# Splitting the down products of the shared groups of an FFN into three single-pass products

## What is computed

```python
x = x + 0.5 * ffn(layernorm(x))
x = x + attention(layernorm(x))        # 16 heads of 64, rotary and Fourier terms
x = x + 0.5 * ffn(layernorm(x))        # same weights again

def ffn(x):                            # N = 4096 tokens, E = 8 experts, top 2, 2 shared groups
    scores = softmax(x @ gate_w.T)
    comb = top-2 weights per token, with an expert's capacity of 1280 tokens
    g, u = x @ we_gate[e].T, x @ we_up[e].T          # every expert on every token, inner size 128
    y = sum_e comb[:, e] * ((silu(g) * u) @ we_down[e].T)
    shared = (silu(x @ ws_gate.T) * (x @ ws_up.T)) @ ws_down.T    # inner size 2 x 128
    return y + shared
```

## Time and profile before

| | |
|---|---|
| median of 3 runs | 1273.29 us (1272.16 to 1274.07) |
| profiled execution: its time | 1275.4 us |
| profiled execution: its span | 1273.6 us |
| granted clock of TensorE, share of full | 0.995 |
| first FFN, with attention's first steps | about 18 to 231 us of the span |
| attention | about 231 to 1084 us |
| second FFN | about 1084 to 1273.6 us |

### The profile page before, as it was taken

The page is one execution under the profiler, slowest core; times in us unless marked ns, Lnnn a source line. Parts: engine busy times, 40 slices in busy tenths (PEclk is TensorE's granted clock), DMA queues, the critical chain, the costliest instruction groups (busy, mean ns, idle before and its releaser), DMA issues.

```text
span 1273.6 us, 20947 instructions
## 1 busy us (share of the span) xinstructions
PE 1229.2 (97%) x7346; PEld 780.9 (61%) x7346; DVE 955.6 (75%) x1443; ACT 627.9 (49%) x917; POOL 896.2 (70%) x652
## 2 busy tenths in 40 slices
PE   4999999899999999999999999999999987999998
PEld 3666666556666566666666666666666644666665
DVE  6656777778888888888888888888787865656632
ACT  3444522455555546455556555555555552443422
POOL 0443346788998898898898899889889932543353
PEclk9999999999999999999999999999999998999999
DMA  5353150132333333232323232323232310443150
GB/s 169 134 183 91 43 150 17 33 66 54 70 58 67 61 64 64 63 65 59 69 60 68 60 68 60 68 57 70 51 77 52 76 19 19 141 142 108 43 158 17
DMA packets 118677, 95.35 MB, mean 75 GB/s; under 512 B 75760, under 2 KB 85008, under 8 KB 118320
## 3 DMA queue, kind: packets, MB, share of 16 engines
q1 hardware_dynamic: 118064, 93.75, 30.2%
q10 hardware_dynamic: 512, 0.26, 0.1%
HBM read 57.53 MB, written 2.88 MB: 47 GB/s over the span
## 4 chain that ended last, share of the span: by engine, by line
PE 86%; issue 4%; POOL 4%; DVE 3%; DMA 1%; ACT 1%; SPq 0%; POOLq 0%; DVEq 0%; ACTq 0%
PE banks L1156 16%; PE banks L453 15%; PE banks L1135 13%; PE banks L466 10%; PE banks L1074 6%; PE banks L994 5%; PE banks L1172 5%; PE banks L1140 4%; PE banks L1181 4%; PE banks L1002 3%; POOL work L1428 2%; PE banks L1113 1%; POOL turn L1418 1%; PE banks L415 1%; PE banks L408 1%
## 5 line engine op out<-in xcount | busy, mean ns | idle before, releaser
L1006 DVE TENSOR_REDUCE neg_max<-banks 128x2 f32<-128x1024 f32 x256 | 305.1, 1226 | 11.0 <-PE banks L994 6.2
L1256 ACT ACTIVATE work<-banks 128x1024 f32<-128x1024 f32 x256 | 262.4, 1026 | 93.8 <-PE banks L1140 77.6
L1156 PE MATMUL banks<-work 128*64 128x512 f32 x1024 | 233.8, 598 | 2.0 <-ACT work L1256 1.1
L1428 POOL TENSOR_TENSOR work<-work 128x1024 f32<-128x1024 f32 x64 | 159.6, 2494 | 81.4 <-PE banks L1156 81.3
L1418 POOL TENSOR_TENSOR turn<-turn,side_turned 128x512 f32<-128x512 f32 x128 | 163.7, 1301 | 29.8 <-DMA side_turned<-side 29.6
L1412 POOL TENSOR_TENSOR turn<-turn,fenc 128x512 f32<-128x512 f32 x128 | 162.8, 1291 | 2.0 <-DVE side L1327 2.0
L1423 POOL TENSOR_TENSOR qk_l<-turn,qk_h 128x512 fp32r<-128x512 f32 x128 | 161.8, 1285 | 2.8 <-ACT qk_h L983 2.8
L1156 PEld LDWEIGHTS banks<-work 128*64 128x64 f32 x1024 | 68.0, 136 | 135.0 <-issue 109.9
L1348 DVE TENSOR_TENSOR work<-work 128x1024 f32<-128x1024 f32 x64 | 105.4, 1647 | 38.2 <-PE banks L1156 38.2
L807 POOL TENSOR_TENSOR o_raw<-o_raw,work 128x512 f32<-128x512 f32 x52 | 66.9, 1289 | 89.8 <-DVE o_raw L723 89.7
L807 POOL TENSOR_TENSOR work<-work 128x512 f32<-128x512 f32 x44 | 56.5, 1292 | 96.7 <-DVE work L723 51.7
(11 more groups left out here) (177 smaller groups left out, 2459.3 us busy)
## 6 DMA issues: line engine op xcount, KB each, us to landing
work<-share SPq DMA_DIRECT2D x32, 1024.0 KB, 9.4
side_turned<-side SPq DMA_DIRECT2D x256, 128.0 KB, 3.1
rec_all<-rec_d SPq DMA_DIRECT2D x128, 128.0 KB, 3.0
x_tok<-in_x SPq DMA_DIRECT2D x8, 256.0 KB, 6.5
out<-x_tok SPq DMA_DIRECT2D x8, 256.0 KB, 9.4
work<-in_w_gate_up SPq DMA_DIRECT2D x1, 1280.0 KB, 7.2
work<-in_w_qk SPq DMA_DIRECT2D x1, 1024.0 KB, 9.7
den_d<-den_rows ACTq DMA_DIRECT2D x64, 4.0 KB
```

Of the source, the lines that this page charges most:

```text
L1006: return nc.vector.tensor_reduce(neg_max[:, g % 2, qt::DH], of, AX.X, ALU.max, negate=True)
L1156: ins = nc.tensor.matmul(o_bank(g)[OWN[h], :], v_all[:, kt, n * DH:(n + 1) * DH], pt[:, g % 2, kt, h * T:(h + 1) * T], start=(kt == 0), st ...
L1256: nc.scalar.activation(pt[:, g % 2, kt, :], S[kt].rearrange("p h q -> p (h q)"), ACT.Exp, scale=QSCALE).then_inc(s["probs"], 1)
L1428: nc.gpsimd.tensor_tensor(pt[:, g % 2, 2, :], pt[:, g % 2, 2, :], pt[:, g % 2, 3, :], ALU.add).then_inc(s["second_sum"], 1)
```

## The change

In units 20, 21, 30, 31, ..., 70, 71 of both FFNs (`split(i)`: batch 2 or later, shared group; 12 units in each FFN) the down product is made of three float32r products in place of one float32 product. ScalarE copies `hid(i)` to its high part `hid_hi[:, g]` (`hid_high`), GpSimd subtracts it from `hid(i)` for the low part `hid_lo[:, g]` (`hid_low`), and `down(i)` waits for the low part. ScalarE's copy stands right behind `silu(i)` in its queue and waits for `gated(i)`. The high part lies in the buffer `shift`, the low part in the third set of `qk_h`, both of them attention's. The down weights of the two shared groups are split once, at unit 9 of the first FFN, ScalarE making the high part and VectorE the low one. Attention's high part of its second head pair gets a wait for the down products that still read the low part's buffer.

```diff
@@ -53,6 +53,7 @@
 JOIN_NORM_AT = {p: (n,) for n, p in enumerate([p for p in range(26, 60) if p % 8 in (0, 1, 2, 6)], 1) if n < LN_STAGES}
 JOIN_TOKENS_AT, JOIN_FRONTS_AT, JOIN_LOGITS_AT = 61, 62, 63
 FOURIER_AT = 17
+DOWN_SPLIT_AT = 9
 
 
 def ffn_units():
@@ -100,6 +101,8 @@
         gu_hi = sb("gu_hi", [P, 2 * GROUPS, P], F32R)
         gu_lo = sb("gu_lo", [P, 2 * GROUPS, P], F32R)
         down_w = sb("down_w", [P, GROUPS, D])
+        down_hi = sb("down_hi", [P, NSH, D], F32R)
+        down_lo = sb("down_lo", [P, NSH, D], F32R)
         gate_w = sb("gate_w", [P, E])
         gate_hl = sb("gate_hl", [P, 2 * CB, GATE_ROWS], F32R)
         qk_hi = sb("qk_hi", [P, PAIRS, QK, P], F32R)
@@ -151,6 +154,7 @@
         qk_l = sb("qk_l", [P, SETS, QK, T], F32R)
         turn = sb("turn", [P, 2, QK, T])
         side = sb("side", [P, QK, T])
+        hid_lo = qk_h[:, 2]
         side_turned = sb("side_turned", [P, QK, T])
         route_room = side_turned[:].rearrange("p q t -> p (q t)")
         routing = lambda n: route_room[:, n * CT * E:(n + 1) * CT * E].rearrange("p (t e) -> p t e", e=E)
@@ -159,6 +163,7 @@
         neg_max = sb("neg_max", [P, 2, P])
         own_rows = sb("own_rows", [P, TT])
         shift = sb("shift", [P, 2, T], F32R)
+        hid_hi = shift
         ones_r = sb("ones_r", [P, P], F32R)
         ones_f = sb("ones_f", [P, 32])
         o_raw = sb("o_raw", [P, 2, T])
@@ -183,6 +188,7 @@
         in_first, in_fourier, in_x0, in_down = sem("in_first"), sem("in_fourier"), sem("in_x0"), sem("in_down")
         consts_ready = sem("consts_ready")
         w_hi_ready, w_lo_ready = sem("w_hi_ready"), sem("w_lo_ready")
+        down_hi_ready, down_lo_ready = sem("down_hi_ready"), sem("down_lo_ready")
         fenc_ps, fenc_ready = sem("fenc_ps"), sem("fenc_ready")
         dve_step = {ph: sem(f"dve_step_{ph}") for ph in ("setup", "f1", "att", "f2")}
         stored = sem("stored")
@@ -318,7 +324,7 @@
         def ffn(tag, last, share_d, follow=None):
             s = {n: sem(f"{tag}_{n}") for n in (
                 "normed", "xn_ready", "xn_first", "xt_ps", "x_hi_ready", "x_lo_ready", "logits_t", "logits_copied", "logits", "shifted", "exps", "masks", "pos",
-                "routed", "turned", "rows_ready", "gate_ps", "up_ps", "silu", "weighted", "gated", "down", "y_copied", "yt_ps", "x_done")}
+                "routed", "turned", "rows_ready", "gate_ps", "up_ps", "silu", "weighted", "gated", "hid_high", "hid_low", "down", "y_copied", "yt_ps", "x_done")}
             listed = tuple(sem(f"{tag}_listed{c}") for c in range(CHUNKS))
             in_share = tuple(tuple(sem(f"{tag}_in_share{n}{h}") for h in range(2)) for n in range(2))
             G, U, Y = (bank[0], bank[1]), (bank[2], bank[3]), (bank[4], bank[5])
@@ -359,6 +365,13 @@
             def experts(i):
                 return sum(1 for b, g in UNITS[0:i] if g >= NSH)
 
+            def split(i):
+                b, g = UNITS[i]
+                return b >= CB and g < NSH
+
+            def splits(i):
+                return sum(1 for n in range(i) if split(n))
+
             def last_of(b):
                 return max(i for i in range(N) if UNITS[i][0] == b)
 
@@ -455,7 +468,10 @@
 
                 def down(i):
                     b, g = UNITS[i]
-                    if g < NSH:
+                    if split(i):
+                        pe.wait_ge(s["hid_low"], splits(i + 1))
+                        pe.wait_ge(down_lo_ready, 1)
+                    elif g < NSH:
                         pe.wait_ge(s["gated"], i + 1)
                     else:
                         pe.wait_ge(s["weighted"], experts(i + 1))
@@ -463,8 +479,13 @@
                         at_least(pe, s["y_copied"], b - 1)
                         if b == 1:
                             pe.wait_ge(s["rows_ready"], 1)
-                    nc.tensor.matmul(Y[b % 2], down_w[:, g, :], hid(i), start=(i == first_of(b)),
-                                     stop=(i == last_of(b))).then_inc(s["down"], 1)
+                    parts = ((down_w, hid(i)),)
+                    if split(i):
+                        parts = ((down_hi, hid_hi[:, g]), (down_lo, hid_hi[:, g]), (down_hi, hid_lo[:, g]))
+                    for m, (w, h) in enumerate(parts):
+                        ins = nc.tensor.matmul(Y[b % 2], w[:, g, :], h, start=(i == first_of(b) and m == 0),
+                                               stop=(i == last_of(b)))
+                    ins.then_inc(s["down"], 1)
 
                 def transpose_y(b):
                     pe.wait_ge(s["y_copied"], b + 1)
@@ -581,6 +602,17 @@
                     at_least(act, s["gated"], i - 1)
                     nc.scalar.activation(act_g[:, i % 2, :], G[i % 2][:], ACT.Silu).then_inc(s["silu"], 1)
 
+                def hid_high(i):
+                    b, g = UNITS[i]
+                    act.wait_ge(s["gated"], i + 1)
+                    if splits(i) >= NSH:
+                        act.wait_ge(s["down"], first_of(b - 1) + g + 1)
+                    nc.scalar.activation(hid_hi[:, g], hid(i), ACT.Copy).then_inc(s["hid_high"], 1)
+
+                def down_high():
+                    act.wait_ge(in_down, 16)
+                    nc.scalar.activation(down_hi[:], down_w[:, 0:NSH], ACT.Copy).then_inc(down_hi_ready, 1)
+
                 def copy_y(b):
                     act.wait_ge(s["down"], last_of(b) + 1)
                     at_least(act, s["yt_ps"], b)
@@ -589,7 +621,11 @@
                 def period(i):
                     if i < N:
                         silu(i)
+                    if i < N and split(i):
+                        hid_high(i)
                     c, q = chunk(i)
+                    if not last and i == DOWN_SPLIT_AT:
+                        down_high()
                     if not last and i == REST_AT:
                         gate_up_high(act, 1)
                     if batch_at(i, FRONT_AT) is not None:
@@ -738,6 +774,9 @@
                     if i < N:
                         gated(i)
                     c, q = chunk(i)
+                    if not last and i == DOWN_SPLIT_AT:
+                        dve.wait_ge(down_hi_ready, 1)
+                        tt(down_lo[:], down_w[:, 0:NSH], down_hi[:], ALU.subtract).then_inc(down_lo_ready, 1)
                     if not last and i == REST_AT:
                         gate_up_low(dve, 1)
                     if turned_at(i) is not None:
@@ -807,9 +846,16 @@
                     nc.gpsimd.tensor_tensor(tiled, tiled, share[b % 2][:, (g - NSH) // HALF_E, :, (g - NSH) % HALF_E, :],
                                             ALU.mult).then_inc(s["weighted"], 1)
 
+                def hid_low(i):
+                    pool.wait_ge(s["hid_high"], splits(i + 1))
+                    nc.gpsimd.tensor_tensor(hid_lo[:, UNITS[i][1]], hid(i), hid_hi[:, UNITS[i][1]],
+                                            ALU.subtract).then_inc(s["hid_low"], 1)
+
                 for i in range(N):
                     if UNITS[i][1] >= NSH:
                         weighted(i)
+                    elif split(i):
+                        hid_low(i)
                     if follow:
                         follow["gpsimd"](pool, i - N + GROUPS)
 
@@ -980,6 +1026,8 @@
 
             def high(act, g, part):
                 act.wait_ge(s["k_sum" if part == K else "q_sum"], g + 1)
+                if g == 1 and part == K:
+                    act.wait_ge(ffn1["s"]["down"], ffn1["units"] - E)
                 nc.scalar.activation(qk_h[:, sets(g), part], turn[:, g % 2, part], ACT.Copy)\
                   .then_inc(s["k_high" if part == K else "q_high"], 1)
 
```

## The result

The kernel with the change takes 1283.64 us (median of 4 runs, 1282.00 to 1284.47), the one before 1272.80 (4 runs, 1272.16 to 1274.07). The ratio is 1.0081, with a 95% interval of 1.0065 to 1.0097: slower by 0.8%, 10.8 us by the medians. The prediction was 1282.4 us in a range of 1274 to 1287, with 0.75 for slower. The profiled execution took 1284.47 us, 9.1 more than the one before (1275.4).

The account below looks back on a forecast made before the run. TensorE, busy 97% of the span, was taken as the bound, apart from short waits. Terms 6.2 + 1.8 + 1.0 - 0.6 + 0.7 = +9.1 us on 1273.3 gave 1282.4 us, range 1274 to 1287.

Parts of the forecast that it names:

- Part 1: Down products: three float32r products take 0.70 us against 0.86, saving 0.16 each, 3.8 us for 24 if all stays.
- Part 2: Added work: 24 ScalarE copies of 0.63 us and 24 GpSimd subtractions of 1.29, the latter starting 1.47 after `gated(i)`.
- Part 3: Router, units 30/31 and 50/51, both FFNs: exponentials 1.53 us late, then L693 held by GpSimd; +6.2 us for four places.
- G: The start of `gated(i)`, from which the prediction counts times; at the routing place, the start of `gated(31)`.
- Part 4: Norm stages, units 21 and 41, both FFNs: the subtraction holds L271 some 0.45 us; +1.8 us for four places.
- Part 5: Attention's first norm, units 60 and 61, first FFN: L306 held by `hid_low(60)`, TensorE waits for it; +1.0 us.
- Part 6: The rest: units 70/71 of first FFN 0, units 60, 61, 70, 71 of second -0.6, weight split +0.7 us.
- The sum: The forecast's terms over all places added up: +9.1 us.
- late exponentials alone: Rival: GpSimd's new work mostly misses VectorE's operations, a routing place costs 0.65; +2.9 us, 1276.2 us, chance 0.20.

Follow-up runs that it names:

- the first experiment: The changed kernel without GpSimd's 24 subtractions, the third product taking the high part again: 1275.79 us, ratio 1.0024 against the kernel before.
- both causes away: The changed kernel with ScalarE's copy issued one unit later and GpSimd's subtractions left out: 1271.88 us, ratio 0.9984 against the kernel before.
- only the quiet units split: The changed kernel splitting 12 products, shared groups of routing batches last where batches stay split, weights split at unit 19: 1274.52 us, ratio 1.0004.
- the fills: The kernel before with two or four VectorE fills ahead of attention's last norm stage; four: 1276.96 us, ratio 1.0022; single executions 1274.13 to 1276.67 us.

## Why the prediction was right

The time came out 1.2 us above the forecast. Part of that closeness is the baseline: the forecast of the difference was 9.1 us on 1273.3, and the measured one is 10.8 on 1272.8.

**Part 1.** Right. Three products take 0.70 us in the chain of the change, in the second FFN's batch 6, and a float32 one there still 0.86:

```profile
1240.56 0.70 PE banks L486 x3
...
1242.67 0.86 PE banks L486 x2
```

Where nothing waits, a pair of split products gave 0.32 us (second FFN's last two batches: 0.32 and 0.31).

**Part 2.** Right: copies 0.63, subtractions 1.27 to 1.30; from `gated(31)` at 1160.20 to `hid_low` at 1161.63 it was 1.43, predicted 1.47.

**Part 3.** Right, in mechanism and nearly in size: exponentials 1.51 later (1.53), next `gated` 2.74 after G (2.9), masks 3.01 after that (2.99). The doubtful step, that L693 (now L729) meets the subtraction, came out as predicted, and the first experiment tells it from the late exponentials. A place cost 1.49 to 1.88 in place of 1.54; at the one shown, TensorE idles 0.90 us right before the positions and 0.55 a unit earlier, where the forecast had 1 to 2 us in one piece. The rule that was weighed there, of the Trainium skill's "SBUF — State Buffer", section "Who interferes with whom", is that a VectorE instruction with two inputs in SBUF contends with a GpSimd instruction that reads SBUF. The rows shown agree with it: L729, L277, L721 and L723 ended within 0.1 us of GpSimd's operation.

**Part 4.** Right, 1.64 for 1.8. L277 was held 0.29 rather than 0.45. The stage at unit 21 of the first FFN cost 0.67, and about 0.37 of it is in all six other versions of the changed kernel: VectorE's `gated(21)` starts that much late. It is there without subtractions (0.40 with both causes away) and also with only the quiet units split, where no copy stands at units 20 and 21, so neither of the two causes makes it. Its cause I did not find.

**Part 5.** This is the term that was mis-sized: 2.8 in place of 1.0. The part that was reasoned, L306 (now L312) held by `hid_low(60)`, came to 0.94 for 1.15 (TensorE's wait, 2.79 for 1.85). Two things were missing: 0.46 of knock-on from the routing stage before it, and about 1.6 for the fallen clock, which is in all three traces with this wait but, by the fills, need not be in every execution. The 0.16 that `down(60)` keeps comes off. The same section of the Trainium skill, by which a one-input operation contends only in a two-port mode, left room for a term of 0.2. L312 has one full input in SBUF and was held, 2.06 us for 1.11, and L282, a TENSOR_SCALAR too, 1.28 for 0.17. The trace doesn't show the mode that they run in.

**Part 6.** Units 70/71 of the first FFN and the last two batches of the second came as taken (+0.16 for 0, −0.64 for −0.6). The weight split at unit 9 cost 0.57 for 0.7, through VectorE as foreseen: `1.45` us for L779's 128x256 beside GpSimd. In the traces of four experiments with the same code it took 0.42 us and cost nothing, in one (without subtractions) 1.41 us and cost 0.40: it is held in some executions and not in others.

The sum is 2.2 below the ledger, 1.8 of it from part 5. Of the rivals, *late exponentials alone* is what the first experiment made, 1275.8 for the 1276.2 worked out for it. Term by term it fits less well: that sum had 0.65 for a routing place, and in the trace the two of the second FFN cost 0.63 and 0.70, those of the first 0.94 and 1.02, and all places together 3.6 in place of 2.9.

## What to carry to other kernels

When work goes to an engine that seems idle, look up which small operations of another engine are under way at that moment, and which of them end in a wait of the bounding engine. A saving of 0.16 us in each of 24 products was never worth a hold of up to 1.2 us at a place where the bounding engine waits already. And before work is moved out of one engine's way, work out where it lands: two of my versions moved it from one hold into another.

## What was not expected of the hardware

TensorE's granted clock went to its lower level behind a single wait of 2.08 to 3.16 us, in the changed kernel after 34 us at 1.00 with TensorE busy 87% of them, and cost 1.3 to 1.6 us each time. The same wait of 2.08 us did it in one execution and not in the next; with 1.85 it was never seen in five traces. So a wait of this length in front of dense products can have a price beside its own, and a single profile cannot tell whether it is paid in the other executions.
